# Mixture-of-experts stage of a two-layer network: unequal groups of blocks, and rows that carry their own way back

## The reference

```
x = x + 0.5 * L0_ffn(layernorm(x))        # base product plus 8 low-rank experts, softmax gates, all used
x = x + L0_attn(x)                        # a Mamba2 layer: projection, conv of 4 taps, scan over time, 4 heads
x = x + 0.5 * L0_ffn(layernorm(x))
x = x + 0.5 * L1_ffn(layernorm(x))        # 8 experts, top 2, and a shared expert
x = x + L1_attn(layernorm(x))             # linear attention, 16 heads of 8, keys summed over a batch
x = x + 0.5 * L1_ffn(layernorm(x))
```

```
scores = softmax(x @ gate_w.T);  top 2 of 8 experts by score;  w = scores at these two, else 0
g, u = halves of x @ gate_up[e].T (2 x 176);  expert_out[e] = (silu(g) * u) @ down[e].T
out = sum_e w[e] * expert_out[e] + sigmoid(x @ shared_expert_gate.T) * shared(x)
```

## Time and profile before

| | |
|---|---|
| median of 3 runs | 963.09 us (961.82 to 971.63) |
| span of the profiled execution, first to last instruction | 869.2 us |
| median less that span | 93.9 us |
| TensorE, VectorE, ScalarE, GpSimd busy | 806.7, 647.6, 518.5, 526.1 us |
| mean granted TensorE clock | 0.988 of full speed |
| indirect DMAs: scatters, gathers, sends | 128, 48, 115 |

### The profile page before, as it was taken

How to read it: one execution, slowest core, us unless ns; L and a number is a source line. 1 busy time by engine, 2 the same in 40 slices (tenths; PEclk the granted TensorE clock), 3 DMA queues, 4 the chain that set the end, 5 groups by cost and what they waited for, 6 DMA issues and landing times.

```text
span 869.2 us, 16114 instructions
## 1 busy us (share of the span) xinstructions
PE 806.7 (93%) x4810; PEld 613.1 (71%) x4810; DVE 647.6 (74%) x2260; ACT 518.5 (60%) x1057; POOL 526.1 (61%) x610
## 2 busy tenths in 40 slices
PE   7999999999999999999989998899899899999893
PEld 6668586757768578677777676686677675785772
DVE  5397688898586866778767958899999588576435
ACT  3887757667777876766756544467473356354241
POOL 3159474668544475683666254876637775757753
PEclk9999999999999999999999999999999999999997
DMA  9920000000101111120122112212212241241333
GB/s 302 397 111 2 1 2 1 2 11 31 34 13 38 43 46 32 49 71 26 40 77 76 53 58 79 71 45 87 63 41 73 71 143 44 81 142 56 97 117 121
DMA packets 62069, 61.81 MB, mean 71 GB/s; under 512 B 7835, under 2 KB 53531, under 8 KB 61771
## 3 DMA queue, kind: packets, MB, share of 16 engines
q1 hardware_dynamic: 52387, 40.94, 15.4%
q0 software_dynamic: 9312, 19.17, 6.9%
q10 hardware_dynamic: 288, 0.67, 0.3%
HBM read 27.46 MB, written 33.30 MB: 70 GB/s over the span
## 4 chain that ended last, share of the span: by engine, by line
PE 35%; DVE 22%; POOL 16%; issue 13%; DMA 6%; ACT 6%; SPq 1%; DVEq 0%; POOLq 0%; ACTq 0%
PE psum L564 6%; PE psum L833 6%; POOL sent_y L1836 5%; PE psum L853 4%; POOL sorted_l L1795 3%; DVE xs L1333 2%; POOL sorted_x L1795 2%; PE psum L644 2%; PE psum L783 2%; PE psum L768 2%; PE psum L773 2%; DVE l_place L1308 2%; DMA sorted_l<-m_cv,r_slot 1%; ACT f_xn L1437 1%; PE psum L688 1%
## 5 line engine op out<-in xcount | busy, mean ns | idle before, releaser
L1836 POOL DMA_INDIRECT sent_y<-e_y,l_to x115 | 111.9, 973 | 62.4 <-DVE e_y L1293 33.3
L833 PE MATMUL psum<-gu_w,e_sx 128*128 x368 | 125.2, 464 | 2.6 <-DVE e_y L1293 1.2
L1795 POOL DMA_INDIRECT sorted_l<-m_cv,r_slot x80 | 77.5, 969 | 44.5 <-issue 21.0
L853 PEld LDWEIGHTS psum<-d_w,e_h 88*128 88x128 f32 x736 | 91.4, 191 | 17.8 <-issue 13.9
L853 PE MATMUL psum<-d_w,e_h 88*128 x736 | 99.2, 278 | 3.6 <-ACT e_h L1442 1.2
L1442 ACT ACTIVATE e_h<-psum 88x512 f32<-88x512 f32 x96 | 54.2, 572 | 63.6 <-PE psum L564 61.6
L1622 ACT ACTIVATE e_h<-psum 128x352 f32<-128x352 f32 x96 | 42.6, 450 | 79.4 <-PE psum L833 79.1
L833 PEld LDWEIGHTS psum<-gu_w,e_sx 128*128 128x128 f32 x368 | 63.8, 190 | 31.9 <-issue 11.2
L1289 DVE TENSOR_TENSOR e_h<-e_h,psum 128x352 f32<-128x352 f32 x96 | 47.6, 501 | 32.7 <-ACT e_h L1622 32.1
L1823 POOL DMA_INDIRECT c_y<-sorted_y,r_slot x48 | 48.4, 1009 | 29.1 <-DMA sorted_y<-e_y 11.9
L1722 POOL TENSOR_TENSOR m_seg<-w_scan,m_dt 128x512 f32<-128x512 f32 x32 | 36.3, 1135 | 47.0 <-PE psum L712 38.7
(11 more groups left out here) (246 smaller groups left out, 2088.5 us busy)
## 6 DMA issues: line engine op xcount, KB each, us to landing
m_cv<-sorted_l SPq DMA_DIRECT2D x55, 130.0 KB, 2.2
sorted_l<-c_y SPq DMA_DIRECT2D x10, 512.0 KB, 14.8
c_y<-sent_y SPq DMA_DIRECT2D x20, 256.0 KB, 4.0
e_sx<-sorted_x SPq DMA_DIRECT2D x33, 128.0 KB, 2.2
sorted_y<-e_y SPq DMA_DIRECT2D x33, 128.0 KB, 1.9
sorted_l<-c_y SPq DMA_DIRECT2D x5, 471.0 KB, 14.5
xs<-in_x SPq DMA_DIRECT2D x8, 256.0 KB, 7.0
sorted_x<-c_y SPq DMA_DIRECT2D x4, 512.0 KB, 14.4
```

Of the source, the lines that this page charges most:

```text
L833: last = e.matmul(two.banks[j].tile[:, 0:2 * IEXP], e_xT[k % 4][:, j * P:(j + 1) * P], gu_w[:, bass.ds(which[j] * (2 * IEXP), 2 * IEXP)], ...
L853: last = e.matmul(bank.tile[:, j * P:(j + 1) * P], e_hT[s][0:IHALF, (2 * j + c) * P:(2 * j + c + 1) * P], d_w[:, bass.ds(which[j] * (2 * D ...
L1795: e.indirect_dma_start(out=sorted_l[SENT_GROUPS.index(g)] if g in SENT_GROUPS else sorted_x[n], out_offset=bass.IndirectOffsetOnAxis(ap=r_ ...
L1836: e.indirect_dma_start(out=sent_y[n], out_offset=bass.IndirectOffsetOnAxis(ap=l_to[n][:, 2 * t + j:2 * t + j + 1], axis=0), in_=e_y[k % 4] ...
```

## The change

The 16 block-layers form six groups of 4, 2, 2, 4, 2 and 2 instead of eight of 2. `MAXT` is 39 tiles in 20 pairs for a group of four, 23 in 12 for a group of two. All groups now use one way: every row is 130 floats, 128 of data, one destination row number, one score (half of the softmax weight). GpSimd writes destination (`place`) and, for the second choice, score into the rows before each four scatters; the score of the first choice is written by VectorE in `gates`. Rows that no token uses carry a spare destination, filled once at the start in 14 transfers. The result of a pair is evicted by ScalarE, a tile at a time, times the score in its row; each tile is sent by an indirect DMA to its destinations; SyncE loads a block's results in one transfer (two for the last two blocks), and `combine` is two plain adds. The gathers, `l_place`, `l_to` and the stores in sorted order are gone. Rings: `g_xn` 6 deep (was 4), `e_sx` 6 deep (was 4). The rings by group stay two deep. The load of pair k wants pair k-6 sent. All due times are new, and so is the order of the feed-forwards (`ORDER`). The gates have a semaphore of their own for their weights. The attention's `o_qT` and `o_o` share memory with `m_seg`, so they want the last Mamba chunk to be done.

```diff
-PRES, KEPT = 2, 4
+PRES, KEPT = 2, 6
...
-GB = 2
...
-NT = GB * TILES_PER_BLOCK
-MAXT = (TOPK * NT * P + E1 * (P - 1)) // P
-PAIRS = -(-MAXT // 2)
...
-SENT_GROUPS = (3, 4, 5, 6, 7)
...
-SLID = 4
+SIZES = (4, 2, 2, 4, 2, 2)
+GROUPS = range(len(SIZES))
+START = [0, *accumulate(SIZES)]
+GROUP_OF = [g for g in GROUPS for _ in range(SIZES[g])]
+NT = [n * TILES_PER_BLOCK for n in SIZES]
+MAXT = [(TOPK * n * P + E1 * (P - 1)) // P for n in NT]
+PAIRS = [-(-n // 2) for n in MAXT]
+PAIR0 = [0, *accumulate(PAIRS)]
+PAIR_OF = [(g, t) for g in GROUPS for t in range(PAIRS[g])]
...
+MAXT = [(TOPK * n * P + E1 * (P - 1)) // P for n in NT]
...
+SXS = 6
...
+EMPTY_ROWS = 15
...
-FIRST = [-6.0, 20.1, 58.2, 69.3, 100.4, 125.5, 150.6, 175.7]
-MAMBA = [16.3, 41.4, 66.5, 91.6, 116.7, 141.8, 166.9, 192.0]
-CHUNK_AT = [29.3, 29.3, 29.3, 29.3, 29.3, 29.3, 29.3, 29.3]
+FIRST = [-586.1, 150.16, -75.28, 301.66, 254.59, 74.26, 337.46, 291.16]
+AGAIN = [134.28, 291.96, -376.44, -231.77, -133.67, -194.21, 346.31, -144.89]
+MAMBA = [182.39, 187.84, -370.07, -257.59, 148.79, -521.53, 489.38, 225.3]
+CHUNK_AT = [281.16, 451.38, -307.13, -98.9, 144.67, -134.17, 36.08, 16.77]
...
+TAP_STEP = -4.55
+FOLD_AT = 40.13
+FINISH = [331.98, -304.8, 166.75, -1223.94, -193.64, 137.7, -472.13, -107.73]
...
+SORTED = [354.01, 868.73, 157.16, 191.32, 403.13, 888.23]
+PAIRED = [487.11, 249.52, -74.32, 214.11, 778.33, 487.23]
+PACE = [21.0, 12.18, 20.09, 10.37, 40.59, 47.62]
+SENDS = [-213.22, 672.05, 912.71, 524.3, 785.12, 773.23]
...
+ORDER = [(0, 0), (0, 1), (0, 2), (0, 3), (1, 0), (0, 4), (1, 1), (1, 2), (0, 5), (0, 6), (1, 3), (1, 4), (0, 7), (1, 5), (1, 6), (1, 7)]
...
+        sorted_x = [nc.dram_tensor(f"sorted_x{g}", [MAXT[g] * P, SENT], F32, kind="Internal").ap() for g in GROUPS]
+        sent_y = [nc.dram_tensor(f"sent_y{g}", [SPARE + TOPK * NT[g] * P, DM], F32, kind="Internal").ap() for g in GROUPS]
         x_tiles = d["x"].rearrange("(t p) c -> p t c", p=P)
         out_tiles = out.rearrange("(t p) c -> p t c", p=P)
...
         def stored(k):
-            g, t = divmod(k - 4, PAIRS)
-            if g in SENT_GROUPS:
-                return f"sent{k % 4}", sent(k % 4, k - 3)
-            return f"sy{k % 4}", 16 * (plain(g) * PAIRS // 4 + t // 4 + 1) if k >= 4 else 0
+            return f"sent{k % 4}", sent(k % 4, k - 3)
...
-                yield (T + 6.6, 2.8, ("g_logits", i + 1), ("w_late", 16 * 4), ("c_add", GB * (g - 1)),
-                       ("gather0", gathered(0, GB * (g - 1))), ("gather1", gathered(1, GB * (g - 1))), ("r_rank", g - 1), ("g_exp", i - 1))
+                yield (T + 6.6, 2.8, ("g_logits", i + 1), ("w_gates", 16), ("c_add", START[max(g - 1, 0)]), ("r_rank", g - 1), ("g_exp", i - 1))
...
-                on.wait_ge("c_add", GB * (g - 1))
-                for c in range(2):
-                    on.wait_ge(f"gather{c}", gathered(c, GB * (g - 1)))
+                on.wait_ge("w_gates", 16)
+                on.wait_ge("c_add", START[max(g - 1, 0)])
...
+                own(e.tensor_scalar(score[0], inverse, 0.5, None, ALU.mult))
+                e.scalar_tensor_tensor(score[1], inverse, 0.5, runner, ALU.mult, ALU.mult).then_inc(*S.up("g_score"))
...
                 e.tensor_tensor(h, h, banks.tile("e_gu", k)[:, 0:m, IEXP:2 * IEXP], ALU.mult).then_inc(*S.up("e_h"))
-                yield T + 12.0, 0.42, ("e_down", k + 1), stored(k)
-                on.wait_ge("e_down", k + 1)
-                on.wait_ge(*stored(k))
-                e.tensor_copy(e_y[k % 4][:, 0:m, :], banks.tile("e_y", k)[:, 0:m * P].rearrange("p (j c) -> p j c", c=DM)
-                              ).then_inc(*S.up("e_y"))
...
-            def send(n, t):
-                nth, g = n * PAIRS + t, SENT_GROUPS[n]
-                k = g * PAIRS + t
-                yield (PAIR[g][t] + 5.0, 0.35, (f"sx{k % 4}", expert_loads(k)), ("r_expert", g + 1),
-                       ("sent_to", nth))
-                on.wait_ge(f"sx{k % 4}", expert_loads(k))
-                on.wait_ge("sent_to", nth)
-                settled()
-                for j in range(pair_tiles(t)):
-                    rows = l_sx[k % 4][:, j, :]
-                    last = e.scalar_tensor_tensor(l_place[:, j:j + 1], rows[:, DM + 1:DM + 2],
-                                                  l_key[n][:, 2 * t + j:2 * t + j + 1], rows[:, DM:DM + 1], ALU.not_equal, ALU.add)
-                own(last)
-                settled()
-                tiles = slice(2 * t, 2 * t + pair_tiles(t))
-                e.tensor_tensor(l_to[n][:, tiles], l_place[:, 0:pair_tiles(t)], empty[:, tiles],
-                                ALU.max).then_inc(*S.up("sent_to"))
                 yield None
...
+                y = c_y[i % 2]
+                behind = len(PAIR_OF) if GROUP_OF[i] == GROUPS[-2] else 0
+                for nth, (t0, m) in enumerate(parts(i)):
+                    yield T + 8.0 + 2.0 * t0, 0.2 + 0.28 * m, ("s_res", i + 1), results(i, nth), ("e_y", behind)
                     on.wait_ge("s_res", i + 1)
-                    on.wait_ge(*landed)
-                    for k in range(TOPK):
-                        for j in tiles:
-                            last = e.scalar_tensor_tensor(x[:, j, :], y[:, k, j, :], r_score[g % 2][:, k, j0 + j:j0 + j + 1],
-                                                          x[:, j, :], ALU.mult, ALU.add)
-                        if k == 0:
-                            own(last)
-                            settled()
-                    if half == 0 and i == ROUNDS * NBLK - 1:
+                    on.wait_ge(*results(i, nth))
+                    tiles = slice(t0, t0 + m)
+                    own(e.tensor_tensor(y[:, tiles, 0, :], y[:, tiles, 0, :], y[:, tiles, 1, :], ALU.add))
+                    settled()
+                    last = e.tensor_tensor(x[:, tiles, :], x[:, tiles, :], y[:, tiles, 0, :], ALU.add)
...
+                on.wait_ge("e_down", k + 1)
+                on.wait_ge(*stored(k))
+                for j in range(m):
+                    last = e.activation(e_y[k % 4][:, j, :], banks.tile("e_y", k)[:, j * P:(j + 1) * P], ACT.Copy,
+                                        scale=e_sx[k % SXS][:, j, DM + 1:DM + 2])
+                last.then_inc(*S.up("e_y"))
                 yield None
...
+                order = [(m, k) for m0 in range(0, blocks, 2) for k in range(TOPK) for m in range(m0, min(m0 + 2, blocks))]
+                for nth, (m, k) in enumerate(order):
+                    four, i = FOURS0[g] + nth, START[g] + m
+                    read = [landed(FOURS0[g] + order.index((m, 0)))] if k else []
+                    before = read + ([landed(four - 2)] if four > 1 else [])
+                    rows = g_xn[i % KEPT]
+                    for half in range(2):
...
+                            on.wait_ge("zeros", 16 * sum(EMPTY_LOADS))
+                            for signal in before:
+                                on.wait_ge(*signal)
+                            tiles = slice(m * TILES_PER_BLOCK, (m + 1) * TILES_PER_BLOCK)
+                            if k:
+                                e.tensor_copy(rows[:, :, DM + 1], r_score[n][:, tiles])
+                            e.tensor_copy(rows[:, :, DM].bitcast(U32), place[:, k, tiles]).then_inc(*S.up("place"))
+                            on.wait_ge("place", four + 1)
+                        for j in (2 * half, 2 * half + 1):
+                            t = m * TILES_PER_BLOCK + j
                             e.indirect_dma_start(
-                                out=sorted_l[SENT_GROUPS.index(g)] if g in SENT_GROUPS else sorted_x[n],
-                                out_offset=bass.IndirectOffsetOnAxis(ap=r_slot[n][:, k, t:t + 1], axis=0),
-                                in_=given(i)[:, j, :] if g in SENT_GROUPS else g_xn[i % KEPT][:, j, :], in_offset=None).then_inc(*S.up(signal, 16, ROWS))
-                yield None
...
+            def send(g, t):
+                k = PAIR0[g] + t
+                for j in range(pair_tiles(g, t)):
+                    yield SEND[g][t], 1.25, ("e_y", k + 1)
                     on.wait_ge("e_y", k + 1)
-                    on.wait_ge("sent_to", n * PAIRS + t + 1)
                     e.indirect_dma_start(
-                        out=sent_y[n], out_offset=bass.IndirectOffsetOnAxis(ap=l_to[n][:, 2 * t + j:2 * t + j + 1], axis=0),
+                        out=sent_y[g], out_offset=bass.IndirectOffsetOnAxis(ap=e_sx[k % SXS][:, j, DM:DM + 1].bitcast(U32), axis=0),
                         in_=e_y[k % 4][:, j, :], in_offset=None).then_inc(*S.up(f"sent{k % 4}", 16, ROWS))
                 yield None
...
+            def empty_rows(g, q):
+                yield MAMBA[0] + 10.0, 0.5, ("empty", 1)
+                on.wait_ge("empty", 1)
+                k = min(EMPTY_ROWS, MAXT[g] - q * EMPTY_ROWS)
+                r = q * EMPTY_ROWS * P
...
-                T = PAIR[g][t]
-                if g in SENT_GROUPS:
-                    nth = SENT_GROUPS.index(g)
```

(15 more changed lines are left out.)

456 lines of the change are left out of this document (165 added, 291 removed).

## The result

The changed kernel took 986.8 us (median of 4 runs, 981.6 to 992.1), the kernel before 966.3 beside it: a ratio of 1.019 [1.014, 1.023]. It is slower, and the forecast of 925 us missed, range and all.

What follows compares the result with a forecast made beforehand. TensorE, busy 806.7 of 869.2 us, was taken as nearly full, with 103 us of stalls after the start. Tiles -24, end -1 and stalls -13 gave a span of 831, plus 93.9 kept: 925 us, range 892 to 966.

Steps and rivals of the forecast that it cites:

- -24 for the tiles: Expert matmuls and transposes on TensorE: 14 fewer tiles at 1.71 us each, 23.9 us, mostly on the path.
- -13 within -52 to +34 for the stalls: TensorE's idle and filler time after the start, 103 us: an eighth goes, 13 us; ends -52 and +34.
- VectorE's 92 us: VectorE's busy time falls from 648 to 556 us, not saved by itself but shortening its queue.
- if `ones` takes the freed time: Sign of being wrong: TensorE filler takes the freed time; `ones` plus idle after 50 us was to fall from 103 to 90.
- The base of the sum: The 963.09 us median stands 93.9 us above the profiled span of 869.2; that difference was kept unchanged.
- ScalarE's eviction, 0.41 us each: Scaled eviction of 170 expert tiles moves to ScalarE: 70 us of busy time, 35 at the lower bound.
- The price 0 for the move: Moving the eviction to ScalarE was costed at 0 us of kernel time, between -3 and +10.
- Spread evenly that is covered: GpSimd's extra sends and small copies, +20 on 526 us busy, are hidden if even; uneven in the first 550 us.
- my 357: First expert matmul moves from 250.53 to about 357 us, after group 0's 32 scatters.
- The first rival: Group 0 of four blocks returns late, `c_add` 4 after about 550 us: 975 to 990 us, chance 0.10.
- The second rival: VectorE, GpSimd and DMA latency fix the end, freed 24 us become filler or idle: 954 to 972 us, chance 0.11.
- The third: New due times and lighter VectorE take back half the stalls after the start: 887 us, chance 0.13.

Runs made afterwards that it cites:

- e11: The changed kernel with all scatters and sends replaced by plain DMAs, so nothing is sorted or returned, on a slow chip: 879.6 us, 0.906.
- e12: The kernel before with its 291 data-dependent DMAs replaced by plain ones, on a slow chip: 861.3 us, 0.890.
- e9: The changed kernel run again without edits, on a slow chip: 984.5 us, 1.013 against the kernel before.
- e14: The changed kernel run a third time without edits, on a slow chip: 992.6 us, 1.028 against the kernel before.
- e13: The changed kernel in eight groups of two blocks, with the old due times and plain DMAs for scatters and sends, on a slow chip: 888.3 us, 0.919.
- the eight twos: The changed kernel with eight groups of two blocks and the due times of before: 971.8 us, 1.013; once more 978.2 us, 1.009.
- e1: The kernel before, unedited, profiled again: 957.1 us, 1.000; its span was 962.3 us.
- e15: Separate small kernel: TensorE, ScalarE and VectorE signal in a ring beside GpSimd's DMAs, slow chip; beside 48 indirect DMAs a 2.31 us round took 40.7.
- e10: The changed kernel in eight groups of two with the old due times, second run, on a slow chip: 978.2 us, 1.009.
- e5: The changed kernel with its 170 sends replaced by plain DMAs, scatters kept, on a quick chip: 914.7 us, 1.043.
- e6: The changed kernel with its 128 scatters replaced by plain DMAs, sends kept, on a quick chip: 885.4 us, 1.013.
- e4: The changed kernel with the scaled eviction back on VectorE, new due times kept: 1011.3 us, 1.058.
- the ring: Separate small kernel, three engines signalling in 2.3 us rounds beside stretches of 24 indirect DMAs, slow chip: 21.9 us lost in a row, 1.2 with waits.

## Why the prediction was wrong

**The step that failed is that the freed work comes off the path: -24 for the tiles, and -13 within -52 to +34 for the stalls.** Without addresses, so without the slow chips' extra time, the changed kernel takes 879.6 us and the kernel before 861.3 (e11, e12): +18 us where the sum had -38. With addresses it was +20.5, +14.9 and +25.6 (first run, e9, e14). Nearly the whole miss is in these terms. By the windows above, TensorE's need fell by 15.7 us and filler plus idle rose by 33.7, the upper bound of the term for the stalls; 30.9 of that is filler. Of the 33.7 the way back by tile brought 18.3 (e12 to e13), groups and due times 15.4 (e13 to e11). Filler stands where the planner sees TensorE wait, and the planner had it: by the expectations above its ends are 864.4 us for the kernel before, 886.9 for the eight twos and 872.8 for the changed kernel, beside 861.3, 888.3 and 879.6 measured with plain DMAs. The prediction read the old trace and never asked the planner for the new end. Which dependence of the way back makes the planner wait is not settled. VectorE's 92 us bought nothing: no group of the earlier trace rows had TensorE wait for VectorE for more than 3.6 us, 7.2 in all, and the prediction never asked which wait of TensorE would end earlier.

**The tiles.** The arithmetic was right: 340 matmuls on `gu_w`, and from e13 to e11 TensorE's need falls by 20.4 us (from e12 to e13, with as many tiles, it had risen by 4.7, which I had at nothing). "Worth nothing only where the planner fills the hole with `ones` again" is what happened, and the prediction's own sign of being wrong, "if `ones` takes the freed time"; 638 of them where 406 stood, and `ones` and idle time after the first 50 us at 127.8 (e11) where about 90 was forecast:

```profile
L524 PE MATMUL psum<-ones 128*128 128x128 f32 x638 | 90.3, 283 | 7.3 <-POOL ones L1747 2.7 <-issue 1.1 <-ACT m_cv L1430 1.0
```

**The base of the sum was wrong in kind, and right in size by luck.** "The 963.09 us median stands 93.9 us above the profiled span ... and I keep the difference." The 94 us are not overhead around the span. They lie inside it, in an execution unlike the one I read: on slow chips indirect DMAs hold TensorE up (e1, e12, e15). It was to be priced like a stall: what is in it, and does the change touch it? On slow chips the sum of it came out the same, 106 us for the kernel before and 984.5 - 879.6 = 105 for the changed one, in which two moves cancel: the eight twos pay 978.2 - 888.3 = 90 us (e10 and e13 are from two slow chips on which the kernel before took 969.6 and 967.0), and groups of four with the new due times 15 more, which eats what they gain with plain DMAs, 888.3 to 879.6 us. The number of indirect DMAs hardly changes (298 for 291, 312 in the eight twos); the longest unbroken row is 32 in e9 and 22 in e1. On quick chips the two kernels may not pay alike: e5 and e6 make some 49 us for the changed kernel, an estimate, where the kernel before has some 13 between 874.1 and e12's 861.3 (an estimate too, from two chips).

**ScalarE's eviction, 0.41 us each.**

```profile
L1547 ACT ACTIVATE e_y<-psum,e_sx 128x128 f32<-128x128 f32 x170 | 53.1, 364 | 90.6 <-PE psum L819 48.7 <-remote 32.0 <-issue 9.6
L1539 ACT ACTIVATE e_h<-psum 128x352 f32<-128x352 f32 x88 | 39.3, 454 | 49.7 <-PE psum L799 38.6 <-remote 7.5 <-issue 3.2
```

0.36 us by its mean and 0.31 of busy time each (53.1/170), 53 us in place of 70; two that follow each other take 0.63 (809.04). ScalarE's sum is 524.6 us, below my 553, because the new order needs 62 table loads instead of 86, 31 us less, which I had not counted. The price 0 for the move was not measured by itself; e4 speaks for it, in its own new order: with the move taken back the ratio is 1.058, against 1.013 to 1.028 of the changed kernel. The Trainium skill, "ScalarE: Activation LUTs", "Rules for kernel authors", gives a plain multiply to VectorE. By the instruction alone the traces agree by little, 344 ns against 364; by the time of the kernel the measurement went for ScalarE. The 0.29 us behind another, an estimate worked out from the page's figures, was close to the 0.31.

**VectorE and GpSimd.** VectorE 556.8 us as forecast. 170 sends at 0.99 us. Four scatters and the small write behind them take 5.3 us (796.83 to 802.15), at 0.20 us a write. "Spread evenly that is covered" failed where the prediction had said the cover could: GpSimd has 42.0 busy of 50 us in 300 to 350, and the first expert matmul comes at 377.53, 20 us after my 357: the 32 scatters begin at 300.8 instead of 291.6, take 70 us instead of 66, and 7 us follow for landing, load and transposes, which I had left out.

**The first rival, a late first group, gave 975 to 990 us, and 986.8 came.** Its number is no merit (its own +15 to +30 on 963 would have made 978 to 993). It predicts that groups of four lose against twos by themselves; with plain DMAs groups of four and new due times win 9 us (e11 against e13, two slow chips). `c_add` 4 came at 496.8 us, within the 500 that I had forecast and far before this rival's 550. What scatters and sends on GpSimd do cost is another thing than a late queue: they hold up TensorE while they run, in both kernels. **The second rival** had the mechanism: the freed tiles turn into filler, which they did. Its 954 to 972 us had no room for a change that adds more than it frees. **The third** had no part.

## What to carry over

When a kernel's own time and its profiled span differ by more than a per cent or two, find out what the difference is before costing anything: the trace may be of another execution than the times, and a constant that you carry over can be the very thing that a change moves. Where a kernel comes with a planner, ask it for the new end before you forecast: here it had the changed kernel 8 us later, not 38 earlier. Work taken off a busy engine is saved only where the wait behind it ends earlier too. Count the longest unbroken rows of indirect DMAs on GpSimd, not only their number and busy time; on a slow chip 24 with a wait for landing after every fourth cost 1.2 us in the ring where 24 in a row cost 21.9. To tell one engine's loss from the others' order, replace the suspect by something of the same size without its peculiarity (a plain DMA of the same tile) and then put it beside a ring that doesn't depend on it.
